# A CIN and MLP recommender kernel: another head, and other plans for the first three quads

## The reference

```python
e = jnp.stack([tbl_0[ids[:, 0]], ..., tbl_38[ids[:, 38]]], axis=1)      # (512, 39, 16)
X0 = Xi = e
for W, b in ((W0, b0), (W1, b1), (W2, b2)):                            # 128 outputs each
    Wr = W.reshape(128, 39, Xi.shape[1])
    Xi = jnp.einsum('hjk,bjd,bkd->bhd', Wr, X0, Xi) + b[None, :, None]
    res.append(Xi.sum(axis=2))
h = jnp.concatenate([*res, dense_ctx], axis=1)                         # (512, 400)
h = relu(h @ W_top1 + b_top1); h = relu(h @ W_top2 + b_top2); y = h @ W_top3
```

## Time and profile before

| what | us |
|---|---|
| median of 3 runs (lowest, highest) | 701.95 (701.53, 703.83) |
| the profiled execution's own time | 706.17 |
| its span | 704.3 |
| TensorE busy | 673.2 (96%) |
| ACT, DVE, POOL busy | 542.5, 472.5, 462.2 |

### The profile page before, as it was taken

The page is one execution under the profiler, slowest core; times in us unless marked ns, Lnnn a source line. Parts: engine busy times, 40 slices in busy tenths (PEclk is TensorE's granted clock), DMA queues, the critical chain, the costliest instruction groups (busy, mean ns, idle before and its releaser), DMA issues. The chain is left out here.

```text
span 704.3 us, 10103 instructions
## 1 busy us (share of the span) xinstructions
PE 673.2 (96%) x2631; PEld 487.2 (69%) x2631; DVE 472.5 (67%) x954; ACT 542.5 (77%) x1939; POOL 462.2 (66%) x445
## 2 busy tenths in 40 slices
PE   4598969999999999999999999999999999999998
PEld 4565747777777777777777777777777777776443
DVE  6237447777787878778777777778877777887000
ACT  3247666989898888888888889898989898998003
POOL 6756566888878777777888878787878555322000
PEclk9688998999999999999999999999999999999999
DMA  5664031313131312212131313131313140300000
GB/s 205 212 189 99 11 85 8 94 7 95 6 95 6 95 8 69 33 48 52 29 72 15 84 9 93 7 95 7 94 8 96 5 143 28 144 2 2 0 1 0
DMA packets 103772, 41.40 MB, mean 59 GB/s; under 512 B 86961, under 2 KB 90033, under 8 KB 103074
## 3 DMA queue, kind: packets, MB, share of 16 engines
q1 hardware_dynamic: 98594, 39.47, 21.5%
q0 software_dynamic: 5120, 1.29, 2.1%
HBM read 11.29 MB, written 2.59 MB: 20 GB/s over the span
## 5 line engine op out<-in xcount | busy, mean ns | idle before, releaser
L443 ACT ACTIVATE prod<-ps_y,xt 128x128 f32<-128x128 f32 x1792 | 494.3, 429 | 83.1 <-PE ps_y L688 77.3
L686 PE MATMUL ps_y<-w_hi,x_hi 128*128 128x512 f32 (+1 forms) x640 | 313.8, 490 | 1.8 <-DVE x_lo L514 1.7
L687 PE MATMUL ps_y<-w_lo,x_hi 128*128 128x512 f32 (+1 forms) x640 | 250.8, 392 | 0.0
L688 PE MATMUL ps_y<-w_hi,x_lo 128*128 128x512 f32 (+1 forms) x640 | 250.6, 391 | 0.0
L348 POOL TENSOR_TENSOR prod<-prod 128x512 f32<-128x512 f32 x128 | 165.4, 1292 | 119.6 <-ACT prod L443 117.4
L558 DVE SCALAR_TENSOR_TENSOR prod<-ps_y,xt,prod 128x128 f32<-128x128 f32 x576 | 165.6, 344 | 51.6 <-PE ps_y L688 51.3
L322 POOL DMA_INDIRECT rows<-in_table,index x160 | 154.4, 965 | 38.8 <-issue 32.7
L686 PEld LDWEIGHTS ps_y<-w_hi,x_hi 128*128 128x128 f32 x640 | 121.7, 190 | 56.0 <-issue 24.9
L565 DVE TENSOR_REDUCE prod<-prod 128x128 f32<-128x1536 f32 x64 | 112.1, 1751 | 69.8 <-ACT prod L443 60.1
L687 PEld LDWEIGHTS ps_y<-w_lo,x_hi 128*128 128x128 f32 x640 | 121.8, 190 | 50.6 <-issue 26.6
L343 POOL TENSOR_TENSOR room<-room 117x512 f32<-117x512 f32 (+1 forms) x105 | 135.3, 1290 | 18.2 <-DMA room<-room 18.1
(11 more groups left out here) (77 smaller groups left out, 237.6 us busy)
## 6 DMA issues: line engine op xcount, KB each, us to landing
room<-room SPq DMA_DIRECT2D x80, 234.0 KB
room<-room SPq DMA_DIRECT2D x48, 78.0 KB
emb_room<-rows SPq DMA_DIRECT2D x180, 5.0 KB
rows<-in_table,index POOLq DMA_INDIRECT x160
g_all<-in_L_rec_W SPq DMA_DIRECT2D x1, 2496.0 KB, 9.8
room<-room SPq DMA_DIRECT2D x16, 156.0 KB
w2t_dram<-g_all SPq DMA_DIRECT2D x1, 2496.0 KB
room<-w2t_dram SPq DMA_DIRECT2D x1, 2496.0 KB, 9.0
```

Source lines behind the costliest of these rows:

```text
L443: ins = nc.scalar.activation(prod[:, SLOT[k] + m // 2, :, m % 2], ps_y[:, g % YBANKS, m * H:(m + 1) * H], ACT.Copy, scale=xt[:, q % 2, ti, ...
L686: nc.tensor.matmul(y, hi, w1_hi[:, cols], start=True, stop=False)
L687: nc.tensor.matmul(y, hi, w1_lo[:, cols], start=False, stop=False)
L688: nc.tensor.matmul(y, lo, w1_hi[:, cols], start=False, stop=True).then_inc(y_made, 1)
```

## The change

- PACKED_FROM goes from 1 to 4: the rows of quads 1 to 3 are laid out like quad 0's (4 DMAs, POOL repeats on 32 partitions, 16 transposes); packed ones start with quad 4.
- The dictionaries become a `Plan` for each quad: quads 0, 1 and 2 have their own, 3 and later the one that quads 1 and later had (STEADY). POOL's gathers are drawn from one list that runs on through the quads; only quads 0 and 1 are gathered ahead of tile 0, and repeat_rows(1) goes between tile 0's adds.
- The head's transposes stand in one list: W1's first six groups, W0, the rest of W1, W2, dense. W1 is loaded in 4 parts and W2 in 2, ahead of the rows' lay_out; `base` and W0 are loaded by ACT. W2's groups 2, 5 and 8 are copied by DVE. dense goes straight to its tile, without DRAM.
- W0's symmetric sum is one DVE operation over 39 x 39, a padding copy and six strided copies.
- Quad 0's first tile: ACT copies its 128 columns of x0 first; TensorE moves them by matmuls with a selection matrix (`pick`, for xa) and with shifted columns of the identity (six windows), DVE multiplies from PSUM, and TensorE sums the seven chunks of 128 columns; x1 is split for this tile alone.
- The other three tiles of quad 0 (384 columns) are shared and cut by DMAs of SP (shares, windows 1, 3, 5) and ACT (windows 2, 4, 6), multiplied by DVE between tile 0's groups and summed by TensorE in tile 0, after groups 2 to 7; turn_rows(1) comes after group 8 instead of 4.

```diff
-PACKED_FROM = 1
+PACKED_FROM = 4
...
+STEADY = Plan(multiplied={(0, 0): [2], (0, 1): [3], (1, 0): [4], (1, 1): [5], (2, 0): [6]}, ahead={(3, 1): [0, 1]},
+              summed={(0, 2): 0, (0, 5): 1, (0, 8): 2, (1, 1): 3, (1, 8): 4, (2, 8): 5, (3, 2): 6},
+              repeated=(1, 1), turned=(2, 4), kept=(2, 6),
+              gathers={(0, 1): 2, (1, 1): 2, (2, 1): 4, (3, 0): 1, (3, 1): 1})
+PLANS = [
+    Plan(multiplied={(1, 1): [0, 1], (2, 0): [2], (2, 1): [3, 4, 5], (3, 0): [6]}, ahead={},
+         summed={(2, 0): 0, (2, 3): 1, (2, 6): 2, (2, 9): 3, (3, 1): 4, (3, 3): 5, (3, 5): 6},
+         repeated=(2, 1), turned=(3, 1), kept=(3, 3),
+         gathers={(0, 0): 2, (0, 1): 5, (1, 0): 1, (1, 1): 2, (2, 1): 1, (3, 1): 4}),
+    Plan(multiplied={(0, 0): [0], (0, 1): [1, 2], (1, 0): [3], (1, 1): [4], (2, 0): [5], (2, 1): [6]}, ahead={(3, 1): [0]},
+         summed={(0, 6): 0, (1, 0): 1, (1, 2): 2, (1, 8): 3, (2, 2): 4, (2, 7): 5, (3, 2): 6},
+         repeated=(2, 1), turned=(3, 0), kept=(3, 1),
+         gathers={(0, 1): 2, (1, 1): 3, (2, 1): 2, (3, 0): 1, (3, 1): 3}),
+    Plan(multiplied={(0, 0): [1], (0, 1): [2, 3], (1, 0): [4], (1, 1): [5], (2, 0): [6]}, ahead={(3, 1): [0, 1]},
+         summed={(0, 2): 0, (0, 7): 1, (1, 0): 2, (1, 2): 3, (1, 8): 4, (2, 8): 5, (3, 2): 6},
+         repeated=(2, 1), turned=(2, 9), kept=(3, 1),
+         gathers={(0, 1): 3, (1, 1): 4, (2, 1): 4, (3, 0): 1, (3, 1): 2}),
+] + [STEADY] * (QUADS - 3)
+FIRST_SUMMED_AFTER = {2: [0], 3: [1], 4: [2], 5: [3], 6: [4], 7: [5, 6]}
+FIRST_TURNED_AFTER, FIRST_KEPT_AFTER = 8, 9
...
+TURNS = ([("w1", g) for g in range(6)] + [("w0", 0), ("w0", 1)] + [("w1", g) for g in range(6, GROUPS)]
+         + [("w2", g) for g in range(GROUPS)] + [("dense", 0)])
...
+            act.wait_ge(emb_turned, 1)
...
+            nc.scalar.copy(first, turned[:, :, 0, :]).then_inc(first_x0, 1)
+            act.wait_ge(first_xa_moved, 1)
+            nc.scalar.copy(xa[0:REP, 0:P], ps_g[0:REP, 0:P]).then_inc(first_xa, 1)
+            nc.scalar.copy(rest, turned[:, :, 1:, :]).then_inc(x0_made, 1)
+            act.wait_ge(x0_made, 1)
+            for c in range(2, CHUNKS, 2):
+                cut_rest(act, c)
...
+            nc.tensor.matmul(ps_g[0:REP, 0:P], pick[0:XROWS, :], first, start=True, stop=True).then_inc(first_xa_moved, 1)
+            for c in range(1, CHUNKS):
+                ins = nc.tensor.matmul(ps_y[0:REP, (c - 1) // 2, (c - 1) % 2 * P:((c - 1) % 2 + 1) * P],
+                                       ident[0:XROWS, c:c + REP], first, start=True, stop=True)
+                if c % 2 == 0:
+                    ins.then_inc(first_moved, 1)
+            for c in range(CHUNKS):
...
+                ins = nc.tensor.matmul(ps_x1[:, 0:P], w0t[0:r, c, :], bz[0:r, c, 0:P], start=c == 0, stop=c == CHUNKS - 1)
+            ins.then_inc(first_summed, 1)
...
                 scale_and_sum(T, DVE_GROUPS[0])
+                if T == 0:
+                    multiply_rest(3)
+                    multiply_rest(4)
                 scale_and_sum(T, DVE_GROUPS[1])
+                if T == 0:
+                    multiply_rest(5)
+                    multiply_rest(6)
...
                 reduce_early(T)
+                if T == 0:
+                    split_rest_x1()
+                    sum_x1(0)
...
-                    if g == 4 and ti == 3 and q + 1 < QUADS:
+                    if g == (4 if q > 0 else 6) and ti == 3 and q + 1 < QUADS:
                         keep_x1(q + 1)
```

More of the change, by code:

```diff
@@ L1 @@
+import itertools
 from contextlib import ExitStack
@@ L75, with __init__ @@
[L75 to L80, removed]
+class Plan:
+    def __init__(self, multiplied, ahead, summed, repeated, turned, kept, gathers):
+        self.multiplied, self.ahead, self.summed = multiplied, ahead, summed
+        self.repeated, self.turned, self.kept, self.gathers = repeated, turned, kept, gathers
@@ L94, in wait @@
+ACT_TURNS = [n for n, (what, g) in enumerate(TURNS) if what != "w2" or KIND[g] == "A"]
+DVE_TURNS = [n for n, (what, g) in enumerate(TURNS) if what == "w1" or what == "w2" and KIND[g] == "D"]
+W1_PARTS = [slice(FIRST[a] * H, (FIRST[b - 1] + SIZES[b - 1]) * H) for a, b in ((0, 2), (2, 4), (4, 7), (7, GROUPS))]
+W1_WAITS = {0: 0, 2: 1, 4: 2, 7: 3}
+W2_PARTS = [slice(0, FIRST[5] * H), slice(FIRST[5] * H, F * H)]
+W2_WAITS = {0: 0, 5: 1}
+SYM = F + CHUNKS - 1
 def wait(engine, semaphore, value):
@@ L359, in _ @@
                     gather(q, g)
[L360 to L363, removed]
+            further = iter([(q, g) for q in range(2, QUADS) for g in range(GATHERS)])
             def between(q, ti, part):
+                plan = PLANS[q]
+                if (q, ti, part) == (0, 0, 1):
+                    repeat_rows(1)
                 if q + 1 < QUADS:
[L367 removed]
+                    for c in plan.multiplied.get((ti, part), ()):
                         multiply(q + 1, c)
                 if q + 2 < QUADS:
[L370 removed]
+                    if (ti, part) == plan.repeated:
                         repeat_rows(q + 2)
[L372 removed]
+                    for c in plan.ahead.get((ti, part), ()):
                         multiply(q + 2, c)
[L374 to L378, removed]
+                for n, g in itertools.islice(further, plan.gathers.get((ti, part), 0)):
+                    if g == 0:
+                        make_index(n)
+                    gather(n, g)
             for T in range(TILES):
@@ L521, in sum_x1 @@
                                         ALU.add).then_inc(r1_made, 1)
[L523 to L527, removed]
+            for n in DVE_TURNS:
+                what, g = TURNS[n]
+                cols = slice(FIRST[g] * H, (FIRST[g] + SIZES[g]) * H)
+                bank = ps_y[:, n % YBANKS, 0:SIZES[g] * H]
+                if what == "w1":
+                    dve.wait_ge(prep_act, ACT_TURNS.index(n) + 1)
+                    ins = nc.vector.tensor_tensor(w1_lo[:, cols], bank, w1_hi[:, cols], ALU.subtract)
+                else:
+                    dve.wait_ge(prep_tr, n + 1)
+                    ins = nc.vector.tensor_copy(w2_out[:, cols], bank)
+                ins.then_inc(prep_dve, 1)
             dve.wait_ge(laid_out, laid_through(0))
@@ L539, in _, with split_rest_x1 @@
                     dve.wait_ge(first_window[c], 16)
-                nc.vector.tensor_tensor(bz[0:r, c, :], bz[0:r, c, :] if c else x0[0:r, 0, :], xa[0:r, :],
+                else:
+                    dve.wait_ge(first_shared, 16 * SPC)
+                nc.vector.tensor_tensor(bz[0:r, c, P:], bz[0:r, c, P:] if c else x0[0:r, 0, P:], xa[0:r, P:],
                                         ALU.mult).then_inc(z_made, 1)
-            dve.wait_ge(small_ld, 16 * 4)
-            split_x1(0)
-            sum_x1(0)
+            def split_rest_x1():
+                dve.wait_ge(x1_hi_made, 1)
+                nc.vector.scalar_tensor_tensor(out=x1_lo[:, 0, P:], in0=ps_x1[:, P:], scalar=b0_col[:, 0:1],
+                                               in1=x1_hi[:, 0, P:], op0=ALU.add,
+                                               op1=ALU.subtract).then_inc(x1_lo_made, 1)
+            spread(0)
+            for c in range(3):
+                multiply_rest(c)
             def scale_and_sum(T, g):
```

232 lines of the change are left out of this document (137 added, 95 removed).

## The result

The changed kernel takes 719.92 us (718.75 to 720.30, 4 runs) against 701.78 (701.53 to 703.83, 4 runs): ratio 1.0249, interval [1.0226, 1.0272]. I had forecast 694.5, with a range from 686 to 701. Its profiled execution has a span of 718.3 us, 14.0 more than the one before; the other 4 us of the medians' difference of 18 are that the execution profiled before was 4 us longer than its kernel's median, and the one profiled after is not.

The account below looks back on a forecast made before the run. TensorE's work was taken as the bound from 136.28 us on, with gains only ahead of it. Terms -11.6 + 4.5 + 7.2 - 17.4 + 9.8 = -7.5 took 706.17 to 698.7; less 4.2, 694.5 us, range 686 to 701.

Parts of the forecast that it names:

- a: W0's sums, 50 small DVE operations made one long one plus copies: off the path, price 0.
- b: W2 turned in front, hidden in idle time; its load delays quad 0's gathers: +1.0 us, range 0 to +2.
- c: Quad 0's first tile by TensorE: first layer1 at 33.8 us instead of 45.4, range 32 to 36; gain 11.6 us.
- d: Other three tiles' layer0 sums inside tile 0: seven matmuls of 384 columns at 0.64 us each, +4.5 us.
- e: Unpacked rows of quads 1 to 3: 16 transposes take 3.2 us against 0.79, +2.4 per quad, +7.2 us.
- f: New plans' waits and low clock, including a 3.0 us wait for POOL's chunk 1: new loss 9.8 us.
- Sum: Terms total -7.5 us: profiled 706.17 becomes 698.7, less 4.2 for profiled execution against median gives 694.5.
- the 17.4 us: Loss before tile 8 in the old kernel's profile, taken as removed: 8.8 us idle plus 8.6 by low clock.
- The slower one: Rival: POOL's 3.0 us wait for all six windows returns in each of three quads; 704 us, chance 0.10.

Follow-up runs that it names:

- no_w2_load: Changed kernel without W2's load, W1 turned a second time in W2's place: 720.03 us.
- before_unpacked: Kernel before the change with PACKED_FROM 16, so all 15 later quads are unpacked: 765.08 us.
- ahead7: Changed kernel with seven of quad 2's gathers issued ahead of tile 0, later gathers seven places earlier: 713.17 us.
- packed5: Changed kernel with PACKED_FROM 5, so quad 4's rows are unpacked too: 717.26 us.
- rows4_early: Changed kernel with seven gathers ahead, PACKED_FROM 1, and quad 4's rows repeated, turned and kept at the steady plan's earlier places: 697.14 us.

## Why the prediction was wrong

By its steps:

- *a.* Priced at 0 and not 0. TensorE's turning does end in time, at 22.4. But the one long sum takes 2.99 us, and with what follows 4.7, nearly the 5.0 of the 50 small ones; and a gather beside it takes 3.21 us instead of 0.95, so that quad 0's last gather ends 1.7 us later than before.
- *b.* The row turn starts 3.4 us later than before (26.71 for 23.32), not 1.0: 2.4 more. Of the 3.0 us by which SP begins late, 1.7 are W2's load (no_w2_load). The rest I put down to a's gather, by the ends of the last gathers; no run freed that gather.
- *c.* From the start of the row turn to the first layer1 I had 9.5 us and it was 10.9, as the clock stayed at half until 36 us: 1.4 more. First layer1 37.6, outside my 32 to 36; gain 7.8, not 11.6. This 3.8, 2.4 of it from b, is the largest miss ahead of tile 8.
- *d.* Right: 0.65 us of spacing per sum, 0.64 predicted, and tile 1 did not wait for x1.
- *e.* A turn was 3.52 us, predicted 3.2; with the low clock behind it 4.2 more than a packed one (before_unpacked), predicted 2.4. I had counted low clock only behind waits. Of the Trainium skill's two rules that I weighed, the one of "SBUF — State Buffer" (Door 1, cachelines) fits: the weight load of 0.297 us and the pace of 0.22 us are the same at both clocks. The 0.103 us of "TensorE: Matmul & The Clock Gate" (LDWEIGHTS), 1.6 us for sixteen, does not hold for weights read at this stride, which took 3.52. The length of one load, by which I weighed them, tells less than I made of it: contiguous loads of 128 columns last 0.19 us in the trace before (line 686, at full clock), though W1's turns follow one another every 0.12. And that the pace of contiguous turns goes with the clock is shown by W2's, 0.21 us at a granted clock of 0.50 (to 35.9 us in the trace before) and 0.12 behind it. It is not shown by W1's, on which I leaned: the windows have 1.00 for both of their paces. No run varied the stride alone.
- *f.* Up to tile 8 the sum of losses was near: 5.9 us idle and 5.0 by the clock, 10.9 in all, predicted 9.8; their places were not (short waits, none over 1.2 us, and the clock low behind the three turns instead of behind one long wait). **The step that failed is the sentence that quads 2 and 3 have no loss, "since from quad 4 on the code is as before".** I had moved the gathers in my count, and the layout of rows, but had not followed quad 4, whose rows are the first packed ones: late gathers by the new plan, then the 11 to 12 us that SP needs for packed rows, which the earlier trace rows show for quad 1. It costs 13.5 us between tile 8 and tile 13: waits of 7.73, 2.12 and 1.33 us, and low clock. ahead7 brings the first wait to 0.51 us and packed5 to 1.44; rows4_early leaves 0.9 of the 13.5. The waits of layer0 in quad 3 are also what the prediction had named as a sign that it would be wrong.
- *Sum.* The miss of 25.4 us: 7.9 ahead of tile 8 (3.8 of b and c, 1.0 of e, 1.1 of f, 2.0 that I can't place: TensorE is busy that much longer than its terms and the clock give), 13.5 behind it, and 4 from taking off the difference between the profiled execution and the median, which the next kernel's profile did not have. That difference seems to be a loss counted twice. Executions of the kernel before that took 705.5 to 706.5 us, as the profiled one, had a mean granted clock of 0.978, those near 702 one of 0.983, and 0.005 of 704 us is 3.5. So the profile that I took the 17.4 us from had about 3.5 us more to lose than the median execution, by this estimate, and then I took 4.2 off again. No trace of a shorter execution of it is there to show the place.
- *Rivals.* The slower one had the right direction and the wrong place: it put a wait of 3.0 us of POOL for the windows in each of three quads and came to 704. TensorE's waits for those products stayed at 2.1 us or less, and the time is 16 us above it. What decided was the layout ahead of them.

The second mechanism, behind most of ahead7's missing 7 us, was also in the diff: the third plan hands quad 4's x0 over after (3, 1), and the steady plan of quad 3 sums its second chunk as early as (0, 5). rows4_early, which moves only that, gains 5.2 us. Another 1.7 us of ahead7's is low clock from 656.5 to 660 us in its profiled execution, with no wait near, which the changed kernel's does not have; its cause is open.

## What to carry to other kernels

When a schedule gets a special beginning, follow the first unit that goes by the old rules again: its inputs are made under the new plan and its consumer counts on the old one. Of two layouts, one with fewer DMAs and one with fewer matmuls, each is right only where the other resource has slack: packing paid 11 us with early gathers and cost 4 without them. In a kernel bound by TensorE, price its small operations by what the clock does behind them too.

## What the hardware showed that I had not expected

- Sixteen transposes of 32 x 123 took 3.52 us at full clock and 3.55 at half, and in the steady part of before_unpacked each such run was followed by 3.4 us at a granted clock of 0.50, with TensorE never idle.
- A gather issued by POOL during DVE's sum over SBUF data took 3.21 us, not 0.95, and ended 0.83 us after the sum. The Trainium skill, "SBUF — State Buffer", SBUF: two separate sides, says that DVE and POOL share one pair of ports as an exclusive lock, which a DVE operation with two SBUF inputs holds against a POOL operation that reads SBUF, until it ends. The trace agrees with that order: this sum has two SBUF inputs, and beside DVE's sums for w_lo, one of whose inputs is in PSUM, the gathers took 0.93 to 0.98 us. DVE's 50 small sums before, beside which every gather took 0.94 to 1.02 us, and the 13 pieces, which did not help, are not explained by it. Left open.
